# A four-stage decoder on one core: the opening led by the last key tile, other places of steps, no identity products ahead of the feed forward's norm

## What is computed

```python
x = latent_attention(x, ctx, L0)   # softmax over tokens, add, layer norm
x = x + softmax(Q K' / sqrt(128)) V Wo + bo            # L1, 77 keys
for layer in range(6):                                 # L2, 16 heads of 64
    tn = ln(t, norm_g, norm_b)
    t = mha(tn, tn, sa_kv, sa_q, sa_ow, sa_ob, mask) + t
    tn = ln(t, norm_g, norm_b)
    t = mha(ctx, tn, ca_kv, ca_q, ca_ow, ca_ob, src_mask) + t
    tn = ln(t, pre_g, pre_b)
    t = t + relu(tn @ w1 + b1) @ w2 + b2
x = latent_attention(x, ctx, L3)
```

## Time and profile before

| | |
|---|---|
| median of 3 runs | 1040.86 us (1040.49 to 1041.8) |
| profiled execution, its time / its span | 1041.94 / 1039.9 us |
| PE, PEld busy | 1018.5 us (98%), 683.0 us (66%) |
| DVE, ACT, POOL busy | 715.5 (69%), 801.0 (77%), 407.7 (39%) |
| largest line on PE | L1104 score products, 26% of the chain |

### The profile page before, as it was taken

One profiled execution on the slowest core, in us unless ns is written; L12 is line 12 of the kernel. 1 busy time (PEld: TensorE's weight loads), 2 busy tenths in 40 slices (PEclk: granted clock), 3 DMA queues, 4 the chain that ended last, 5 costly groups with the idle time before them and its releaser, 6 DMA issues.

```text
span 1039.9 us, 22180 instructions
## 1 busy us (share of the span) xinstructions
PE 1018.5 (98%) x5980; PEld 683.0 (66%) x5980; DVE 715.5 (69%) x4485; ACT 801.0 (77%) x3527; POOL 407.7 (39%) x419
## 2 busy tenths in 40 slices
PE   8899999999999999999999999999999999999996
PEld 6655567766568766558875557876646876655885
DVE  4666787567778566778665578766678856677955
ACT  4787998667988676899676799867798868689852
POOL 4233543233544233454333354323354424354432
PEclk9999999999999999999999999999999999999999
DMA  8412000004000003200002200000400000000000
...
DMA packets 31957, 32.89 MB, mean 32 GB/s; under 512 B 4008, under 2 KB 27730, under 8 KB 31058
## 3 DMA queue, kind: packets, MB, share of 16 engines
...
...
HBM read 30.86 MB, written 0.52 MB: 30 GB/s over the span
## 4 chain that ended last, share of the span: by engine, by line
PE 95%; DVE 2%; issue 1%; ACT 1%; DVEq 0%; POOL 0%; POOLq 0%
PE S L1104 26%; PE T L1116 13%; PE sum L1160 12%; PE W L916 9%; PE sum L1130 8%; PE W L940 4%; PE W L971 4%; PE W L858 3%; PE W L895 3%; PE W L878 2%; PE W L873 2%; PE W L935 2%; PE W L837 2%; PE W L849 2%; PE W L827 1%
## 5 line engine op out<-in xcount | busy, mean ns | idle before, releaser
L1405 ACT ACTIVATE Pb<-Pb,mn 128x128 f32<-128x128 f32 (+1 forms) x1536 | 560.6, 370 | 51.6 <-DVE mn L1640 51.4
L722 POOL TENSOR_TENSOR Pb<-Pb,rsum 128x512 f32<-128x512 f32 (+2 forms) x336 | 325.0, 969 | 552.2 <-DVE rsum L1648 552.2
L1405 ACT ACTIVATION_READ_ACCUMULATOR Pb<-Pb,mn 128x1 f32 x1536 | 293.1, 191 | 0.0
L1640 DVE CUSTOM_DVE_ANT_0 Pb<-S,late_bias 128x128 f32<-128x128 f32 x768 | 175.6, 285 | 125.9 <-PE S L1104 125.0
L1116 PEld LDWEIGHTS T<-ident,Pb 128*128 128x128 f32 (+2 forms) x1296 | 163.3, 147 | 127.4 <-issue 105.1
L1104 PE MATMUL S<-GV,XT 128*128 128x512 f32 x384 | 200.3, 608 | 2.6 <-issue 1.8
L1116 PE MATMUL T<-ident,Pb 128*128 128x128 f32 (+2 forms) x1296 | 196.9, 273 | 0.2
L1658 DVE COPY PT<-T 128x512 f32<-128x512 f32 (+1 forms) x240 | 156.5, 652 | 45.5 <-PE T L1116 44.4
L1640 DVE CUSTOM_DVE_ANT_0 Pb<-S,cross_bias 128x77 f32<-128x77 f32 x768 | 132.3, 232 | 55.7 <-PE S L1104 53.5
L1160 PEld LDWEIGHTS sum<-Vc,PT 128*128 128x128 f32 (+2 forms) x1056 | 131.4, 190 | 21.3 <-issue 18.7
L1160 PE MATMUL sum<-Vc,PT 128*128 128x128 f32 (+2 forms) x1056 | 139.1, 276 | 0.0
...
## 6 DMA issues: line engine op xcount, KB each, us to landing
...
```

The costliest lines, as they stand in the source:

```text
L722: nc.gpsimd.tensor_tensor(rows, rows, r, ALU.mult).then_inc(sem(f"{unit.name}_weights"), 1)
L1405: last = nc.scalar.activation(Pb[:, s, t * w:(t + 1) * w], Pb[:, s, t * w:(t + 1) * w], ACT.Exp, bias=mn[:, s, t:t + 1], scale=-1.0, accum ...
L1640: last = nc.vector.tensor_tensor_reduce(out=Pb[:, s, cols], in0=S_ps[n % 2][:, cols], in1=row_bias, scale=1.0, scalar=3.4e38, op0=ALU.add, ...
```

## The change

`FILL` goes from 3 to 0. Most of the tuples change. The opening is reordered: the last tile of batch 0 (`LATE`) runs through L1's second half, the decoder norm and its transposition (`PRE_X`) ahead of the other three (`OTHERS`), whose `xn` VectorE copies now; batch 1's exponentials, turn and values move from ahead of the ticks into ticks 1, 2 and 4 (`opening`); `PRE_CQ` goes to the end; `base` does GpSimd's scaling in three parts (late tile, then the second root, the three others, at the end batch 1); the early mask products are spread differently on ScalarE; loads change places; the 31 identity products of the opening keep their number and get other places, three of them ahead of the first G and two ahead of the three tiles' `xn`. The helpers get the tiles, the bank and the count as arguments. Cut to its core:

```diff
 LAG = {"out": 3}
-FILL = 3
-CV0_AT = (10, 12, 15, 16, 24, 27)
-CV_AT = (4, 6, 7, 20, 26, 29)
-SELF1_AT = (23, 24, 26, 30)
-SELF0_AT = (18, 18, 26, 29)
-WEIGHTS0_AT = (5, 3, 7, 12, 16, 18)
-WEIGHTS_AT = (20, 23, 30, 32, 33, 33, 35, 35, 37, 37, 40, 40, 43, 42, 45, 45)
-AFTER_S0 = (3, 4, 5, 5, 6, 7)
+FILL = 0
+FIRST_AT = (0, 1, 0, 4, 5, 6, 2)
+OPEN_AT = (0, 1, 3)
+XN1_AT = (6, 7, 9, 11)
+CV0_AT = (14, 17, 19, 20, 25, 31)
+CV_AT = (4, 6, 7, 20, 26, 28)
+SELF1_AT = (23, 24, 26, 32)
+SELF0_AT = (17, 17, 26, 28)
+WEIGHTS0_AT = (3, 2, 5, 10, 14, 16)
+WEIGHTS_AT = (18, 21, 28, 30, 31, 31, 33, 33, 35, 35, 38, 38, 41, 40, 43, 43)
+AFTER_S0 = (3, 4, 8, 8, 9, 10)
 AFTER_S1 = (2, 3, 4, 4, 5, 6)
-AFTER_X0 = (2, 2, 3, 4, 5, 7)
+AFTER_X0 = (2, 2, 3, 4, 5, 6)
 AFTER_X1 = (0, 2, 3, 4, 5, 7)
-LAST_AT = (1, 3, 5, 9)
-FEED0 = ((8, 8, 9, 9), 10, (13, 14, 15, 17))
-FEED1 = ((9, 9, 9, 9), 12, (18, 18, 20, 21))
+LAST_AT = (1, 4, 8, 11)
+FEED0 = ((7, 7, 7, 7), 8, (11, 12, 13, 15))
+FEED1 = ((10, 9, 9, 9), 14, (18, 18, 20, 21))
...
+        self.opening = [[] for _ in range(self.ticks)]
...
             self.last_attention(b, 2 + b, (1, 4, 7, 8, 10, 12))
     def place(self):
-        for b in range(B):
-            self.early[1 + 4 * b].append(("xn", 0, b, 0))
+        kept, turned, values, kept1, values1, turned1, rest = FIRST_AT
+        self.jobs[1 + kept].append(("k", 0, 0, 0))
+        self.jobs[1 + turned] += [("G", 0, 0, 0, 0), ("G", 0, 0, 0, 1)]
+        self.jobs[1 + rest].append(("xn", 0, 0, 0))
+        self.jobs[1 + values].append(("v", 0, 0, 0))
+        self.jobs[1 + kept1].append(("k", 0, 0, 1))
+        self.jobs[1 + values1].append(("v", 0, 0, 1))
+        self.jobs[1 + turned1] += [("G", 0, 0, 1, 0), ("G", 0, 0, 1, 1)]
+        for what, dt in zip(("exps", "turn", "values"), OPEN_AT, strict=True):
+            self.opening[1 + dt].append(what)
+        assert OPEN_AT[2] < XN1_AT[0]
+        self.normalise(1, ("xn", 0, 1, 0), XN1_AT[0:3])
+        self.early[1 + XN1_AT[3]].append(("xn", 0, 1, 0))
         first = [[(kind, 0, i) for kind in ("ck", "cv")] for i in range(3)] + [[("cG", 0, i, r) for r in range(2)] for i in range(3)]
         for events, dt in zip(first, WEIGHTS0_AT, strict=True):
             self.jobs[1 + dt] += events
-        self.self_operands(0, 0, 1, (0, 2, 4, 6))
         for j in range(self.layers):
...
 PRE_TQ = [("tq", 0, i) for i in range(2)]
-PRE = Ring("pre", PRE_CQ + PRE_TQ + [("small", 0)], 3)
+PRE_X = ("late", 0, 0)
+PRE = Ring("pre", PRE_TQ + [("small", 0), PRE_X] + PRE_CQ, 3)
+LATE, OTHERS = slice(TB - 1, TB), slice(0, TB - 1)
 SQUARES = 4
 ON_VECTOR = {"v", "V", "cv", "cV", "fin", "out", "v3", "s3", "p3"}
 def by_vector(ring, event):
-    return event[0] in ON_VECTOR or event[0] == "o" and event[3] % 2 == 0
+    return event[0] in ON_VECTOR or ring is FAST.ring and event == ("xn", 0, 0, 0) or event[0] == "o" and event[3] % 2 == 0
...
             load_rows(bet["L0"], "L0", "beta", sem("rows_in"))
             load_rows(bo1, "L1", "bo", sem("rows_in"))
             load_rows(gam["L0"], "L0", "gamma", sem("rows_in"))
-            load_cross_q(0)
             load_q(0)
-            load_small_rows()
-            load_kv(0)
-            load_cross_kv(0)
             sp.dma_start(norm_g[:], col(a["L2_xattn_norm_g"])).then_inc(sem("norm_in"), 16)
             sp.dma_start(norm_b[:], col(a["L2_xattn_norm_b"])).then_inc(sem("norm_in"), 16)
+            load_kv(0)
+            load_small_rows()
+            load_cross_q(0)
+            load_cross_kv(0)
             load_o(0)
             sp.dma_start(cross_bias[:].bitcast(I32), a["mask_Bx1xS2_if1"].rearrange("b a m -> a b m").broadcast_to([P, B, M]))\
               .then_inc(sem("cross_mask_in"), 16)
...
-            sp.wait_ge(sem("X_biased"), B)
+            sp.wait_ge(sem("X_biased"), B + 1)
...
-            root("start", slice(TB, NT), 2)
...
-            gp.wait_ge(sem("start_norm"), B)
-            for b in range(B):
-                rows = X[:, b * TB:(b + 1) * TB, :]
-                nc.gpsimd.tensor_tensor(rows, XN[:, b * TB:(b + 1) * TB, :],
-                                        gam["L0"][:].unsqueeze(1).broadcast_to([P, TB, E]), ALU.mult)\
+            def base(ts, count):
+                rows, n = X[:, ts, :], ts.stop - ts.start
+                nc.gpsimd.tensor_tensor(rows, XN[:, ts, :], gam["L0"][:].unsqueeze(1).broadcast_to([P, n, E]), ALU.mult)\
...
-                gp.wait_ge(sem("X_scaled"), b + 1)
-                nc.gpsimd.tensor_tensor(rows, rows, bo1[:].unsqueeze(1).broadcast_to([P, TB, E]), ALU.add)\
+                gp.wait_ge(sem("X_scaled"), count)
+                nc.gpsimd.tensor_tensor(rows, rows, bo1[:].unsqueeze(1).broadcast_to([P, n, E]), ALU.add)\
...
-            for b in range(B):
-                root("start", slice(b * TB, (b + 1) * TB), B + b + 1)
+            gp.wait_ge(sem("start_norm"), 1)
+            base(LATE, 1)
+            root("start", slice(TB, NT), 2)
+            base(OTHERS, 2)
+            root("start", LATE, 3)
+            root("start", OTHERS, 4)
+            gp.wait_ge(sem("start_norm"), 2)
+            base(slice(TB, NT), 3)
...
-                    made(ring, [("xn", j, b, 0)], l, fills)
+                    made(ring, [PRE_X if unit is FAST and (j, b) == (0, 0) else ("xn", j, b, 0)], l, fills)
...
                         i = event[3]
                         even = (*event[:-1], 0)
                         fills, halves = [even, event], [bank_of(ring, even), w]
+                        if (j, b, i) == (0, 0, 0):
+                            keep(3, sum_ps)
                         made(ring, [("k", j, b, i), ("tq", j, i)], l, fills)
                         for c in range(TB):
                             p = TB * i + c
...
                     if not unit.wide and event[2:] == (0, 2):
                         for t in range(2 * FILL):
                             nc.tensor.matmul(w[:, t % TB * P:(t % TB + 1) * P], ident[:], ident[:], start=True, stop=True)
+                    tokens = range(TB)
                     if event in unit.norms:
                         pe.wait_ge(sem(f"{unit.name}_norm"), l * len(unit.norms) + unit.norms.index(event) + 1)
                     else:
-                        pe.wait_ge(sem("start_norm"), B + b + 1)
-                    for t in range(TB):
+                        for t in range(2):
+                            nc.tensor.matmul(w[:, t * P:(t + 1) * P], ident[:], ident[:], start=True, stop=True)
+                        pe.wait_ge(sem("start_norm"), B + 2)
+                        tokens = range(TB - 1)
+                    for t in tokens:
                         last = nc.tensor.transpose(w[:, t * P:(t + 1) * P], XN[:, b * TB + t, :], ident[:])
+                elif what == "late":
+                    made(ring, [], l, fills)
+                    pe.wait_ge(sem("start_norm"), B + 1)
+                    last = nc.tensor.transpose(w[:, 0:P], XN[:, TB - 1, :], ident[:])
                 elif what == "h":
                     _, _, b, f = event
                     pe.wait_ge(sem("ff_in"), 32 * n_in)
...
-            pe.wait_ge(sem("x_in1"), 16)
-            turned(X, 1, T_ps[1]).then_inc(sem("A_turned"), 1)
...
+                    pe.wait_ge(sem("x_in1"), 16)
+                    turned(X, 1, T_ps[1]).then_inc(sem("A_turned"), 1)
...
-            def second_turn(b):
-                pe.wait_ge(sem("L1_exp"), b + 1)
-                for t in range(TB):
-                    last = nc.tensor.transpose(T_ps[b][0:M, t * P:(t + 1) * P], P1[:, b, t * M:(t + 1) * M], ident[:])
+            def second_turn(b, ts, bank, count):
+                pe.wait_ge(sem("L1_exp"), count)
+                for t in range(ts.start, ts.stop):
+                    last = nc.tensor.transpose(bank[0:M, t * P:(t + 1) * P], P1[:, b, t * M:(t + 1) * M], ident[:])
...
-            def second_values(b):
-                pe.wait_ge(sem("L1_wT"), b + 1)
-                for t in range(TB):
-                    last = nc.tensor.matmul(T_ps[b][:, t * P:(t + 1) * P], OP[0:M, b, t * P:(t + 1) * P],
+            def second_values(b, ts, bank, count):
+                pe.wait_ge(sem("L1_wT"), count)
+                for t in range(ts.start, ts.stop):
+                    last = nc.tensor.matmul(bank[:, t * P:(t + 1) * P], OP[0:M, b, t * P:(t + 1) * P],
...
-            pre(*PRE_CQ)
-            keep(4, sum_ps)
-            second_turn(0)
+            keep(2)
+            second_turn(0, LATE, sum_ps, 1)
...
-            keep(1, sum_ps)
+            keep(1)
...
-            second_values(0)
-            second_scores(1)
-            pre(*PRE_TQ, ("small", 0))
-            keep(2, sum_ps)
+            second_values(0, LATE, S_ps[0], 1)
+            second_turn(0, OTHERS, T_ps[0], 2)
...
-            keep(4, sum_ps)
-            second_turn(1)
+            pre(*PRE_TQ)
+            second_values(0, OTHERS, T_ps[0], 2)
...
-            second_values(1)
+            second_scores(1)
```

(64 more changed lines are left out.)

52 lines of the change are left out of this document (32 added, 20 removed).

## The result

The changed kernel took 1038.53 us in the median of its runs, and the kernel before, run beside it on the same chip, 1041.87: a ratio of 0.9971 (95% interval 0.9963 to 0.9980), or 3.0 us less on the 1040.86 of the prediction, where 5.5 were forecast. The profiled execution of after took 1038.23 us, with a span of 1036.3.

A forecast was written before the change was run, and what follows sets the result against it. TensorE, busy 1018.5 of 1039.9 us, was taken to bound the kernel. Opening 3.0, layers 0 to 4 2.0 and layer 5 0.5 sum to 5.5 off 1040.86: 1035.4 us, with an eight-in-ten range of 1029.4 to 1039.0.

The forecast's parts named there:

- The identity products: L929, ahead of the feed forward norm's transposes in six layers: 1.34 us each, hiding no wait; 8.0 us if removed alone.
- New waits in the layers: Layers 0 to 4: pauses of 0.5, 0.15 and 0.8 replace 1.34 of products and 0.52 of pauses; gain 0.4 each, 2.0 us.
- the walk: Layer 0's feed forward norm, step by step: rows end at 170.9, TensorE's own work at 170.4, so a 0.5 us pause.
- The wait for the masks: Before a layer's first scores: the 0.17 us pause for masks goes, as three scores in a row become two and one.
- the 0.43: TensorE's pause before the transposes of L923 in each layer: 0.43 us, stays because sums and transposes keep their order.
- The walk's 0.1: TensorE's stretch up to the norm's transposes in layer 0: 0.1 us added for changes between half and whole array rows.
- Layer 5: Last layer, no next layer to load: pauses of 0.3 for the rows and 0.5 for XT; 0.5 us of 1.34 gained.
- The opening: Start of the run through the ninth score, reordered: 3.0 us gained, bounds 1.0 and 4.5.
- The dense part: First to ninth score: gaps of 1.8 us in the old order, about 0.8 in the new; 1.0 gained.
- The way to the first score: Opening up to the first score, at 37.6 for 40.51: 2.9 us earlier, less 0.98 for batch 1's values, so 1.9.
- The page on the port: VectorE and GpSimd in the opening: whichever starts first holds their shared port; opening gain 2.1 or 3.9 us by who follows.
- Rival 4: New pauses let the granted clock fall to 1.2 GHz, some 4.8 us per fall; a fall in six layers gives 1064; chance 0.07.

The follow-up runs named there:

- the kernels with the root first: GpSimd's root of batch 1 put back ahead of bo + beta: in after, ratio 0.9941; in the new opening with old layer numbers and no layer identity products, 0.9902.
- the kernel with fitted products: After, with four, one and four identity products added in its opening's three waits, sized not to overrun them: median 1038.05 us, ratio 0.9959.

## Why the prediction was right and wrong

- **The identity products: right.** "They hide nothing as things stood", 8.0 us for all: the kernel without them gave 8.0 by its trace.
- **New waits in the layers: right in kind, too large.** Forecast 0.5 before the norm's transposes, 0.15 at the third hidden product, 0.8 before the first scores; measured 0.37, none, 0.63. They add to 1.0 and not to 1.45, so a layer gave 0.75 and not 0.4. The score product, the copies and the rows fall as walked: VectorE's rows end at 170.45 + 0.85 = 171.30 and TensorE's own work at about 171.07, 0.4 and 0.7 later than in the walk; 0.44 of either is the later start of the stretch (142.06 for 141.62). Five layers: 3.75 for 2.0. But the new numbers also put 0.97 us ahead of layer 0's transposes, which the sum had at nothing. The wait for the masks went and the 0.43 stayed, as said. The walk's 0.1 for changes between half and whole rows of the array has no row of its own, before or here.
- **Layer 5: right.** With the old opening the last stretch fell by 0.57 us (69.11 for 69.68), for 0.5 forecast; the two waits are 0.36 and 0.27, together 0.2 less than put there. In after it fell by 0.21 only, since the new opening adds 0.36. That I had costed at nothing. All fourteen traces with the new opening wait 0.61 or 0.62 us before the final norm's transposes, the three with the old one 0.25 or 0.26. VectorE stands there for 0.45 us that no wait explains, ahead of its variance step; the cause stays open:

```profile
1012.24 0.17 DVE L1790 TENSOR_SCALAR veps<-mv 128x2 f32<-128x2 f32 x1 [0.45 <-issue]
```

- **The opening: the step that failed.** Forecast 3.0, its bound below 1.0; alone it gave nothing by the medians (ratio 1.0005), and by its trace 0.35 from the first root to layer 0's transposes, which the 0.57 behind them takes back. Two terms of its sum were off, and one thing was not in it.
  1. *The dense part.* I had the old order lose 1.8 us in gaps between the first and the ninth score and the new one 0.8: a gain of 1.0. The waits that the traces name there, first in before, then in after between its first and ninth score, are 0.49 and 0.31 + 0.63 = 0.94: a loss of 0.45.
```profile
48.07 1.16 PE L895 MATMUL W<-kT,wqT 64*128 64x128 f32 x16 [0.49 <-issue]
```
```profile
38.47 1.12 PE L1143 MATMUL S<-GV,XT 128*128 128x512 f32 x2
...
53.25 0.63 PE L962 MATMUL W<-ident,XN 128*128 128x128 f32 x4 [0.31 <-DVE XN L1549]
...
55.80 0.66 PE L1155 MATMUL T<-ident,Pb 128*128 128x128 f32 x4 [0.63 <-POOL Pb L743]
...
57.38 1.13 PE L1143 MATMUL S<-GV,XT 128*128 128x512 f32 x2
```
From the first score to the ninth TensorE takes 16.41 us in all three traces with the old opening and 18.91 or 18.92 in all fourteen with the new one, whatever their clock did earlier. The 2.5 more are batch 1's values (0.99, which the sum had), twelve records for the cross matrices `Gc` (0.98, work that only changes places) and these waits. I had taken differences between modelled ends and next starts for gaps; where no wait is named between two records, no trace shows any of it won. This term alone was 1.45 us too high.
  2. *The way to the first score.* Counted from the first root it came at 23.19 in before; the forecast was 20.6 (37.6 less 17.32 - 0.35); measured were 22.42 in after and 21.3 to 21.4 in the three kernels with the same order on GpSimd and a flag product at 10.3 to 10.4. The chain on GpSimd was seen rightly in kind. That batch 1's rows ended at 23.57, where 23.7 was forecast, is luck: the first root came 0.9 us earlier than the forecast took it (16.05 for 17.32 - 0.35). Counted from that root they took 7.52 and not 6.7: 2.64 behind the end of the second root for 2.0, since GpSimd's addition got in between too, which the prediction had as a bound, and the late tile's two operations took 0.45 each for 0.35. The forecast's 6.7 and 20.6 are what the kernels with the root first show: rows at 6.76, first score at 20.7. The gamma rows landed after 5.8 to 8.7 us in the traces, so behind a wait for them a root that TensorE needs can come late by chance. I priced this order at 0.2 us of the root plus 0.9 of the port and left it in the forecast; undoing it was worth 1.9 by the medians and 0.6 by traces without a fall.
     With 1.45 and 0.7 off, the 3.0 leave 0.85. Two traces with this order and the old numbers show just that: 0.35 and 0.37 behind the first root, and 0.5 ahead of it.
  3. *The clock.* I looked for falls in the layers, where they didn't come in any trace, and took the gap of 0.96 before k as proof that the opening was safe. In after the fall behind 14.28 cost 1.0 us on the way to the flag product (11.40 for 10.37 in the kernel with fitted products, whose trace has no fall). My rows held a warning: the column of the granted clock reads 1.00 from the first microsecond in every trace, also over a start that runs at half pace by its records, so it does not show every slow stretch.
- **The page on the port.** The trace shows VectorE's three rows at 1.67 us where 0.85 is their own time, beside GpSimd's product and addition, each 1.00. The Trainium skill, page SBUF — State Buffer, section Who interferes with whom, has the engine that issues first hold the shared pair for its whole instruction. The trace agrees, if taken instruction by instruction: VectorE's series is three instructions, and GpSimd's addition went in between at 21.97.
- **Rival 4 and its page.** The Trainium skill, page TensorE: Matmul & The Clock Gate, section A second HAM failure mode: psum-queue depth-cycling, told of many small pauses. In the layers three or four waits of 0.17 to 0.63 us a period left the granted clock at 1.00 from 50 to 1020 us in all seventeen traces, as I had argued. The falls that came are behind single longer waits in the opening.

**What stays open.** How much of the medians' shortfall in the opening is the clock's: traces say 1.0 in after and up to 2.3 elsewhere, medians between 0 and 1.2. What makes the start's half pace end earlier or later. And 0.5 of the 0.97 us by which after's dense stretch exceeds that of the new opening with the old numbers (114.61 for 113.64); 0.45 is work moved ahead, twelve records of saq's transpositions for eight.
